# Third stage of a four-block kernel: side work over three banks, probability turning over two, in a new order

## The reference

```python
scores = einsum('bci,bcj->bij', x, x); context = einsum('bij,bcj->bci', softmax(scores), x)   # block 1
mixed = einsum('btd,rde->bte', x, factors) / sqrt(8) + bias                                   # block 2
h = norm_scale * x / (nrm + EPS) * split_scale                                                # block 3
q, k, v = h @ Wq.T, h @ Wk.T, h @ Wv.T      # 8 heads of 64 for q, 2 groups of 64 for k and v
attn = softmax(q k^T / 8); x + (attn v) @ Wo.T
g, u = gate(x) * gate_s, up(x) * up_s; (silu(g) * u) @ down * down_s                          # block 4, inner size 1408
```

## Time and profile before

| what | us |
|---|---|
| median of three runs (lowest, highest) | 1461.83 (1461.3, 1461.9) |
| the profiled execution: its own time | 1460.45 |
| its span | 1458.6 |
| PE, DVE, ACT, POOL busy, share of the span | 95%, 69%, 55%, 51% |
| one batch of block 3 from score to score (batch 3) | 76.6, of it DVE busy 69.67 |

### The profile page before, as it was taken

The page is one execution under the profiler, slowest core; times in us unless marked ns, Lnnn a source line. Parts: engine busy times, 40 slices in busy tenths (PEclk is TensorE's granted clock), DMA queues, the critical chain, the costliest instruction groups (busy, mean ns, idle before and its releaser), DMA issues.

```text
span 1458.6 us, 20717 instructions
## 1 busy us (share of the span) xinstructions
PE 1386.4 (95%) x6864; PEld 1134.4 (78%) x6864; DVE 1010.8 (69%) x2070; ACT 798.1 (55%) x1554; POOL 740.7 (51%) x1008
## 2 busy tenths in 40 slices
PE   5999999988999999999999999799999999999996
PEld 4888877766777877878787887588888888888884
DVE  5888869867989898989898989666242442434333
ACT  4666646647777878786868788632222222213221
POOL 5888646735536465554646455553343424333241
PEclk9999999999999999999999999999999999999998
DMA  6665133241302112121212041430101011010100
GB/s 192 169 174 127 40 101 116 87 130 38 94 4 64 65 44 88 44 87 37 87 28 96 15 121 40 145 138 1 58 1 59 4 54 58 0 58 0 58 29 29
DMA packets 53516, 101.32 MB, mean 69 GB/s; under 512 B 3760, under 2 KB 4784, under 8 KB 53424
## 3 DMA queue, kind: packets, MB, share of 16 engines
q1 hardware_dynamic: 49728, 92.83, 19.1%
q0 software_dynamic: 3696, 7.34, 3.1%
HBM read 70.79 MB, written 25.17 MB: 66 GB/s over the span
## 4 chain that ended last, share of the span: by engine, by line
PE 75%; DVE 13%; POOL 4%; issue 4%; ACT 3%; DMA 1%; SPq 0%; POOLq 0%; DVEq 0%; ACTq 0%
PE context L1889 13%; PE score L2367 11%; PE context L2367 11%; PE context L58 6%; PE score L58 6%; PE context L2395 5%; PE turned L2395 5%; PE score L899 4%; PE turned L1925 4%; PE context L1951 2%; PE context L1953 2%; DVE g_neg_max L1754 2%; PE context L1925 2%; DVE g_q L1677 1%; DVE g_ptl L1770 1%
## 5 line engine op out<-in xcount | busy, mean ns | idle before, releaser
L1413 POOL TENSOR_SCALAR g_prob<-g_prob,g_inv_sum 128x512 f32<-128x512 f32 x256 | 178.0, 697 | 268.9 <-DVE g_inv_sum L1759 268.8
L1548 ACT ACTIVATE g_prob<-score,g_neg_max 128x512 f32<-128x512 f32 x256 | 177.2, 692 | 115.5 <-DVE g_neg_max L1754 113.1
L2143 POOL TENSOR_TENSOR f_hl<-f_hidden,f_hh 128x512 fp32r<-128x512 f32 x88 | 121.9, 1386 | 216.0 <-DVE f_hh L2276 216.0
L1754 DVE TENSOR_REDUCE g_neg_max<-score 128x1 f32<-128x512 f32 x256 | 174.7, 682 | 43.9 <-PE score L58 43.4
L2367 PE MATMUL context<-g_hth,f_w 128*128 128x512 f32 x352 | 137.8, 391 | 2.3 <-ACT f_w L2193 2.2
L2367 PE MATMUL score<-g_hth,f_w 128*128 128x512 f32 x352 | 137.8, 392 | 0.6 <-DVE g_htl L2293 0.5
L2367 PE MATMUL context<-g_htl,f_w 128*128 128x512 f32 x352 | 137.1, 390 | 0.0
L2367 PE MATMUL score<-g_htl,f_w 128*128 128x512 f32 x352 | 137.1, 390 | 0.0
L58 PE MATMUL score<-g_kh,g_q 128*128 128x512 f32 x256 | 123.4, 482 | 10.7 <-ACT g_prob L1548 7.5
L2199 ACT ACTIVATE f_silu<-score,g_bits 128x512 f32<-128x512 f32 x44 | 30.3, 690 | 176.1 <-PE score L2367 176.1
L2199 ACT ACTIVATE f_silu<-context,g_bits 128x512 f32<-128x512 f32 x44 | 30.4, 690 | 174.5 <-PE context L2367 174.5
(11 more groups left out here) (261 smaller groups left out, 3950.6 us busy)
## 6 DMA issues: line engine op xcount, KB each, us to landing
xt<-x_t SPq DMA_DIRECT2D x16, 512.0 KB, 6.9
x_mixed<-x_resident SPq DMA_DIRECT2D x8, 1024.0 KB, 4.4
x_pair<-x_mixed SPq DMA_DIRECT2D x8, 1024.0 KB, 8.2
g_res<-x_mixed SPq DMA_DIRECT2D x8, 1024.0 KB, 6.5
x_attended<-g_res SPq DMA_DIRECT2D x8, 1024.0 KB, 5.1
x_pair<-x_attended SPq DMA_DIRECT2D x8, 1024.0 KB, 5.6
x_resident<-x SPq DMA_DIRECT2D x7, 1024.0 KB, 11.3
factor_sum<-factors POOLq DMA_DIRECT2D x7, 1024.0 KB, 10.8
```

The costliest lines, as they stand in the source:

```text
L1413: nc.gpsimd.tensor_scalar(prob[:, at, :], prob[:, at, :], inv_sum[:, at:at + 1], 1.0, ALU.mult, ALU.mult).then_inc(prob_ready, 1)
L1548: nc.scalar.activation(prob[:, at, :], score[u % 2][:, :], ACT.Exp, bias=neg_max[:, at:at + 1], scale=1.0, accum_out=row_sum[:, at:at + 1] ...
L1754: nc.vector.reduce_max(neg_max[:, at:at + 1], score[u % 2][:, :], AX, negate=True).then_inc(max_ready, 1)
L2143: self.nc.gpsimd.tensor_tensor(self.hl[:, at, :], self.hidden[:, at, :], self.hh[:, at, :].bitcast(F32), ALU.subtract).then_inc(self.hl_re ...
```

## The change

The bank that was the third for turning (`s.output[1]`) becomes the third for side work; turning has two. The order of the names, the shares per step, and some fixed steps are new, and the planner's rule for `earliest` looks back three names instead of two. By hand the new planner ends are: q1 2, v 3, q2 5, q3 8, h0 8, wo0 11, h1 12, wo1 15, h2 15, wo2 18, h3 18, wo3 20, k 23, q0 27, vt 29; wo0 begins in step 9, k in step 21. All steps but 30 and 31 have side work. RESIDUAL goes from (11, 14, 19, 23) to (10, 14, 17, 19), NORM from (19, 20, 28, 29) to (19, 20, 24, 25), ADD is one step behind NORM. CONVERT stays.

```diff
--- before.py
+++ after.py
@@ -1010,25 +1010,25 @@
 
 
 
-NAMES = ["v", "q1", "q2", "q3", "h0", "h1", "wo0", "wo1", "h2", "h3", "wo2", "k", "wo3", "q0", "vt"]
+NAMES = ["q1", "v", "q2", "q3", "h0", "wo0", "h1", "wo1", "h2", "wo2", "h3", "wo3", "k", "q0", "vt"]
 SPLIT = [name for name in NAMES if name[0] != "w"]
-OWN = ("v", "q1", "q2", "q3")
+OWN = ("q1", "v", "q2", "q3")
 IN_LAST = OWN + ("h0", "h1", "h2", "h3")
 
 
 
 FIRST_STATS, FIRST_SCALES = (0, 1, 2, 2), (3, 4)
-STATS = (16, 18, 21, 22)
+STATS = (18, 19, 22, 24)
 SCALES = (31, 0)
-H = (5, 6, 8, 11)
+H = (5, 6, 9, 13)
 CONVERT = (25, 26, 32, 39)
-SHARE, SHARE_AT_END, SHARE_BESIDE_OUT = 8, 7, 3
+SHARE, SHARE_AT_END, SHARE_BESIDE_OUT = 6, 5, 3
 
 LAST_MAP = (0, 1, 2, 3)
 
 PIECES = 3 * IT
 MAP_PIECES = (0, 0, 2, 2, 0, 0, 2, 2)
-STEP_PIECES = [(20, 26, 28, 30)] * 4 + [(20, 28, 30)] * 3
+STEP_PIECES = [(21, 23, 27, 29)] * 4 + [(21, 27, 29)] * 3
 assert sum(MAP_PIECES) + sum(len(steps) for steps in STEP_PIECES) == PIECES
 LOW_COLUMN, LOW_COUNT = 1, 4
 
@@ -1055,7 +1055,7 @@
             name, count = waiting[0]
             cost = 2 if name[0] == "h" or name == "v" else 1
             i = NAMES.index(name)
-            earliest = [end[n] + (2 if n[0] == "w" else 3) for n in NAMES[max(i - 2, 0):max(i - 1, 0)] if n in end]
+            earliest = [end[n] + 3 for n in NAMES[max(i - 3, 0):max(i - 2, 0)] if n in end]
             earliest += {"wo0": [CONVERT[-1] - UNITS + 2], "k": [end.get("h3", 0) + 3],
                          "h0": [H[0] + 2], "h1": [H[1] + 2], "h2": [H[2] + 2], "h3": [H[3] + 2]}.get(name, [])
             if at == 0 and earliest and max(earliest) > u:
@@ -1073,7 +1073,8 @@
 
 
 SHARES, END = side_schedule()
-AHEAD = len(SPLIT) - len(OWN)
+PROLOGUE = [name for name in SPLIT if name not in OWN]
+AHEAD = len(PROLOGUE)
 WO = [END[f"wo{t}"] for t in range(T)]
 RESIDUAL = [at - 1 for at in WO]
 NORM = [WO[1] + 4, WO[1] + 5, WO[3] + 4, WO[3] + 5]
@@ -1086,14 +1087,19 @@
 
 def side_at(b, name):
 
-    return side_use(b, name) % 2
+    return side_bank(side_use(b, name))
+
+
+def side_bank(use):
+
+    return use % 2 if use < AHEAD else 2 - (use - AHEAD) % 3
 
 
 def side_use(b, name):
 
 
     if isinstance(b, int) and b <= 0:
-        return AHEAD + b * len(SPLIT) + SPLIT.index(name)
+        return AHEAD + SPLIT.index(name) if b == 0 else PROLOGUE.index(name)
     j = NAMES.index(name)
     if isinstance(b, int) and b >= B - 1 and name[0] == "w":
         missing = [n for n in NAMES[:j] if n in SPLIT and (b == B or n not in IN_LAST)]
@@ -1103,7 +1109,7 @@
 
 def side_split(b, name):
 
-    return b * len(SPLIT) + (AHEAD + SPLIT.index(name) + 1)
+    return b * len(SPLIT) + (AHEAD + SPLIT.index(name) + 1) if b >= 0 else PROLOGUE.index(name) + 1
 
 
 def side_works(u, first, last, drain):
@@ -1253,8 +1259,8 @@
         obn, omv, ove, ors, oshift = own.obn, own.omv, own.ove, own.ors, own.oshift
         neg_max, row_sum, inv_sum = own.neg_max, own.row_sum, own.inv_sum
 
-        score, side, output = s.score, s.side, s.output[0]
-        turned = [s.turned[0], s.turned[1], s.output[1]]
+        score, side, output = s.score, [s.side[0], s.side[1], s.output[1]], s.output[0]
+        turned = s.turned
         x_loaded = [s.x_first_loaded, sem("x_loaded1")]
         res_loaded, stored = sem("res_loaded"), sem("stored")
         s.attended_stored = stored
@@ -1279,7 +1285,7 @@
 
         def mixed_bank(b, use):
 
-            return (turned if b == B - 1 else side)[use % 2]
+            return turned[use % 2] if b == B - 1 else side[side_bank(use)]
 
         @block.sync
         def _(sp):
@@ -1593,7 +1599,7 @@
                     act.wait_ge(turn_ready, g - TURN_LAG + 1)
                     at = turn_u % T
                     nc.scalar.copy(pth[:, (turn_u // T) % 2, :, at * P:(at + 1) * P],
-                                   blocks_of(turned[(g - TURN_LAG) % 3][:, :])).then_inc(hi_ready, 1)
+                                   blocks_of(turned[g % 2][:, :])).then_inc(hi_ready, 1)
                 for name in side_done(u, first, last, drain, 1):
                     if name in SPLIT:
                         hi_of(b, p, name)
@@ -1757,17 +1763,17 @@
                     at = (u - 1) % 4
                     dve.wait_ge(exp_ready, g)
                     nc.vector.reciprocal(inv_sum[:, at:at + 1], row_sum[:, at:at + 1]).then_inc(inv_ready, 1)
+                if u == END["q0"] + 3 and side_runs("q0", first, last, drain):
+                    lo_of(b, p, "q0", 1)
                 for name in side_done(u, first, last, drain, 2):
                     if name in SPLIT:
                         lo_of(b, p, name, 0 if name == "q0" else None)
-                if u == END["q0"] + 3 and side_runs("q0", first, last, drain):
-                    lo_of(b, p, "q0", 1)
                 turn_u = u - TURN_LAG
                 if not (first and turn_u < 0) and not (drain and turn_u >= 0):
                     dve.wait_ge(hi_ready, g - TURN_LAG + 1)
                     cols = slice(turn_u % T * P, (turn_u % T + 1) * P)
                     at = (turn_u // T) % 2
-                    nc.vector.tensor_tensor(ptl[:, at, :, cols], blocks_of(turned[(g - TURN_LAG) % 3][:, :]),
+                    nc.vector.tensor_tensor(ptl[:, at, :, cols], blocks_of(turned[g % 2][:, :]),
                                             pth[:, at, :, cols].bitcast(F32), ALU.subtract).then_inc(lo_ready, 1)
                 for name in side_done(u, first, last, drain, 1):
                     if name not in SPLIT:
@@ -1835,25 +1841,29 @@
 
         @block.tensor
         def _(pe):
-            def side_bank(use):
-
-                if not (isinstance(use, int) and use < 2):
+            def side_bank_free(b, use):
+
+                if use == AHEAD:
+                    pe.wait_ge(rest.mixed_ready, B * T)
+                elif use > AHEAD and b < B:
+                    pe.wait_ge(side_free, use - 2)
+                elif use >= 2:
                     pe.wait_ge(side_free, use - 1)
 
             def turn_h(b, use, t):
-                side_bank(use)
+                side_bank_free(b - 1, use)
                 pe.wait_ge(h_ready, b * T + t + 1)
                 for k in range(T):
                     cols = slice(k * P, (k + 1) * P)
-                    last = nc.tensor.transpose(side[use % 2][:, cols], h[:, t % 2, cols], s.identity[:, :])
+                    last = nc.tensor.transpose(side[side_bank(use)][:, cols], h[:, t % 2, cols], s.identity[:, :])
                 last.then_inc(side_ready, 1)
 
             def turn_v(b, use):
-                side_bank(use)
+                side_bank_free(b, use)
                 pe.wait_ge(side_hi, side_split(b - 1, "vt"))
                 for t in range(T):
                     cols = slice(t * P, (t + 1) * P)
-                    last = nc.tensor.transpose(side[use % 2][:, cols], v_turned[:, cols], s.identity[:, :])
+                    last = nc.tensor.transpose(side[side_bank(use)][:, cols], v_turned[:, cols], s.identity[:, :])
                 last.then_inc(side_ready, 1)
 
             def split(lh, ll, rh, rl):
@@ -1863,13 +1873,13 @@
 
 
                 use = side_use(b, name)
-                out = mixed_bank(b - 1, use) if name[0] == "w" else side[use % 2]
+                out = mixed_bank(b - 1, use) if name[0] == "w" else side[side_bank(use)]
                 if name[0] == "h":
                     return turn_h(b + 1, use, int(name[1]))
                 if name == "v":
                     return turn_v(b, use)
                 if start == 0:
-                    side_bank(use)
+                    side_bank_free(b, use)
                 if name == "k" and start == 0:
                     pe.wait_ge(side_free, side_use(b, "h3") + 1)
                 if name == "wo0" and start == 0:
@@ -1916,13 +1926,13 @@
                 turn_u = u - TURN_LAG
                 if not (first and turn_u < 0) and not (drain and turn_u >= 0):
                     pe.wait_ge(prob_ready, g - TURN_LAG + 1)
-                    if first and turn_u < 3:
-                        pe.wait_ge(rest.mixed_ready, (B - 1) * T + (1, 2, 4)[turn_u])
+                    if first and turn_u < 2:
+                        pe.wait_ge(rest.mixed_ready, (B - 1) * T + turn_u + 1)
                     else:
-                        pe.wait_ge(lo_ready, g - TURN_LAG - 2)
+                        pe.wait_ge(lo_ready, g - TURN_LAG - 1)
                     for k in range(T):
                         cols = slice(k * P, (k + 1) * P)
-                        mm = nc.tensor.transpose(turned[(g - TURN_LAG) % 3][:, cols], prob[:, turn_u % 4, cols],
+                        mm = nc.tensor.transpose(turned[g % 2][:, cols], prob[:, turn_u % 4, cols],
                                                  s.identity[:, :])
                     mm.then_inc(turn_ready, 1)
                 if not drain:
@@ -1992,7 +2002,7 @@
                 gated.weights_of(pe, 3, with_lo)
```

(9 more changed lines are left out.)

## The result

The changed kernel takes 1482.85 us (median of 4 runs, 1481.19 to 1484.99) against 1461.87 for the kernel before, a ratio of 1.0142, 95% interval 1.0127 to 1.0158: slower by 21 us, nearly twice the 10.9 that the forecast summed up. That is inside the range of eight in ten (1456 to 1484), but only by 1.2, and 1.9 above the forecast's own range of 1465 to 1481. The profiled execution took 1483.15, 22.7 more than that of before.

A forecast was written before the change was run, and what follows sets the result against it. PE was taken as the bound (75.04 of 76.6 us a batch), DVE close behind (69.67). 3 x 0.86 + 3 x 1.78 + 3.0 = 10.9 gave 1471.4 profiled, 1472.7 median; own range 1465 to 1481, eight in ten 1456 to 1484.

The forecast's parts named there:

- The signs: wo0 waiting about 2 us, turns waiting in steps 27 and 0; batches of 78.4 (1 to 3), 77.5 (4 to 6).
- What goes: Five PE waits, at v, the score after step 9, h1 and wo0, h3, wo2, vanish: 3.09 us a batch.
- wo0 in step 9: PE stands 2.07 us before wo0 for the output's last low part, which POOL makes in step 8.
- the 2.80: Time from one DVE maximum to the end of POOL's low part, a term of wo0's wait: 2.80 us.
- DVE's lag at the end: Late DVE makes turns wait for `g_ptl`: 0.73 us in step 27, 1.15 at batch end, 1.88 a batch.
- The piece's transfer: Batches 0 to 3: DVE waits 0.92 us for the third piece's fetch, making the end of batch 2.80.
- rival 4: The clock falls in the new stalls, 1.5 us lost in each of seven batches: 10.5, 1483 us; chance 0.12.
- Batch 7: Score of step 25 comes 3.2 us later behind DVE's lag, before the branch; the batch loses 3.0 in all.
- Batch 0: No wo; stalls of 2.6 us against gains elsewhere: net 0, between -3 and +3.
- Block 4, "and nobody waits for it": Store of the batch before issued some 4 us sooner with nobody waiting for it; block 4 changes 0, within 1.
- The gaps and the banks: Consistent bubbles can mean too few PSUM buffers; by that rule the third side bank wins 3.09 us a batch.
- the prediction's second rule: DVE instructions start only on an empty pipe: plain step 1.51 us, changed kernel near 60 later; forecast rejected it for 1.26.

The follow-up runs named there:

- experiment 2: Changed kernel with POOL's last low part of the output ahead of its normalise in step 8: 1471.88 us, 1.0078 of the kernel before.
- experiment 6: Changed kernel with q2's low part behind the conversion in DVE's step 7: 1501.90 us, 1.0280 of the kernel before.
- experiment 10: Changed kernel with ACT's second norm piece in step 7 instead of 6 and the edit of experiment 6: 1490.29 us, 1.0197 of the kernel before.
- experiment 3: Changed kernel with the statistics five to seven steps sooner (13, 14, 15, 17): 1478.29 us, 1.0130 of the kernel before.
- experiment 4: Changed kernel with half of q0's low part and the count of vt behind `g_ptl` in DVE's step 30: 1475.88 us, 1.0103 of the kernel before.
- Experiment 1: Three side and two turning banks alone, with order, statistics, shares and pieces of the kernel before: 1462.31 us, 1.0010 of the kernel before.
- experiment 5: Changed kernel with the third piece of the next candidates read one step later (28 for 27): 1477.01 us, 1.0108 of the kernel before.
- experiment 11: Changed kernel with only ACT's second norm piece moved from step 6 to step 7: 1480.74 us, 1.0127 of the kernel before.
- experiment 7: Changed kernel with the edits of experiments 2, 3, 4 and 6 together, and the pieces' steps moved too: 1467.48 us, 1.0048 of the kernel before.
- experiment 8: Kernel of experiment 7 with the last batch's weights one to five steps sooner: 1467.91 us, 1.0060 of the kernel before.
- experiment 9: Kernel of experiment 7 without the edit of experiment 6: 1458.07 us over 11 runs, 0.9978 of the kernel before.
- experiment 12: Kernel of experiment 7 with ACT's second norm piece also in step 7: 1462.36 us over 11 runs, 1.0011 of the kernel before.

## Why the prediction was right, and where its sizes were off

The mechanism was right and its sum too small: 10.9 us for 21. That the time still fell inside the range is in part luck. Of what was missing, 4.6 us are the clock, whose rival stood at 0.12, and 1.25 a long issue of two DMAs in batch 1, which the sum had nowhere. The signs came as named, but the batches last 80.8 to 81.1 and 78.4, not 78.4 and 77.5.

**What goes**: right. v, h1, h3 and wo2 start without a bank wait. But the five waits were worth 2.9 a batch by the trace, not 3.09, and small waits of at most 0.1 each, as in steps 8, 9 and 21, which I had counted at nothing, add up to 0.4 to 0.5 in the changed kernel.

**wo0 in step 9**: right in mechanism and size, 1.98 to 2.02 in every batch from 1 to 7 against 2.07. DVE's step 7 took 3.99 (forecast 4.01). Experiments 2, 6 and 10 show the link that holds: POOL's queue, with the normalise ahead of the low part. The forecast had it only as part of the 2.80.

**DVE's lag at the end**: right in kind and place, too small. Step 27 waits 1.19 and 0.15 ahead of it (forecast 0.73), the end 1.89 (2.07 with the piece, 1.15 without; batches 4 to 6 have 0.76 and 1.62). The lag at step 25 was 2.41, forecast 1.84, of which 0.5 comes from step 23, where sum and piece take 2.93, not 2.44: I had the piece at the 0.57 of a pass and took nothing for the instruction ahead. The turn also starts 0.15 behind `g_ptl`, not 0.05, in each of these waits. For batches 4 to 6 I used the demands of four pieces, though they read three, none of them in step 23. Experiments 3 and 4 confirm the two conditions apart from each other: the statistics set step 27, what lies ahead of `g_ptl` in step 30 sets the end.

**The piece's transfer**: 0.92 forecast for batches 0 to 3, 0.4 measured in batches 2 and 3, where DVE itself arrived later. In batch 1 it was 1.7, because the issue of one pair of copies took 2.49 in SP's queue, where the same pair takes 1.24 in batches 0, 2, 3, 4 and 6, and the fetch stood behind it:

```profile
462.74 2.49 SPq L1346 DMA_DIRECT2D g_kl<-g_kl  x2
465.27 0.58 SPq L1160 DMA_DIRECT2D g_h<-down_t  x1
```

**The clock**: rival 4, which I had beside the forecast and not in it, came true in part. Batches 2 and 3 lost 1.6 and 1.7 behind wo0's wait, and batch 7 2.57 in place of 1.22, behind the stall at its branch. (The clock column of batch 7 is 0.98 in some kernels here and 0.96 in others whose stall at the branch is as long, so this part isn't tied to the new waits.) That is 4.6 us of the 12.5 that the sum missed. The rest: batch ends of 1 to 3 2.5, half of it the 1.25 of batch 1; of 4 to 6 1.5; and the terms of "What goes" the remainder.

**Batch 7**: 3.13 in steps 24 and 25 against 3.2. **Batch 0**: 0.15 against 0, by luck. Steps 0 to 6 are 2.3 shorter than before and steps 7 and 8 2.7 longer, and neither was in the forecast.

**Block 4, "and nobody waits for it"**: this step failed, by 2.2 to the good. In the kernel before PE waits in block 4 for weights that were fetched late:

```profile
943.54 0.50 PE L2367 MATMUL context<-g_hth,f_w 128*128 128x512 f32 x1 [2.17 <-ACT f_w L2193]
```

The fetches stand in SP's queue behind the stores of block 3; the changed kernel issues those sooner. Before, then after (last scores of block 3 at 928.3 and 953.1):

```profile
929.99 0.40 SPq L1291 DMA_DIRECT2D x_attended<-g_res  x1
934.38 0.38 SPq L1346 DMA_DIRECT2D g_res<-x_mixed  x1
934.80 0.58 SPq L2112 DMA_DIRECT2D raw_w<-gate_t  x1
```

```profile
945.45 0.40 SPq L1297 DMA_DIRECT2D x_attended<-g_res  x1
949.83 0.38 SPq L1352 DMA_DIRECT2D g_res<-x_mixed  x1
953.85 0.35 SPq L2123 DMA_DIRECT2D raw_w<-gate_t  x1
```

The fetch comes 6.5 behind the last score before and 0.7 behind it after, and the wait is gone in every kernel here with the new order, and stays with the banks alone.

**The gaps and the banks.** Four of the five gaps looked like too few banks, as the Trainium skill (Perfetto Trace Analysis, Optimization Strategy) allows. Experiment 1 gives the third bank and moves the gaps to the turns: by the trace the buffers were one limit, and DVE's lateness the next, worth as much (2.4 of waits for 2.1). As to the prediction's second rule, the section that it names (VectorE: DVE Perf Modes, The DRAIN you can't avoid) says in the same paragraph that a next instruction which isn't held starts earlier; so the 1.26 of a plain DVE step doesn't contradict the Trainium skill, and the 60 us worked out from that rule had no ground.

## What to carry to other kernels

A buffer taken from one stage for another moves the wait, as long as the engine that frees both is late; first ask how late that engine is, step by step. An instruction ahead of a critical one may be filling a wait that is there anyway: moving it behind can cost nearly its whole length (1.36 of 1.39 here), so look up what the critical one waits for before moving anything. Work late in one engine's order can wait on a chain that runs over another queue's older entries, and then reordering that queue is the cure, as with POOL's two instructions here, worth about 11 us.

## What the runs showed of the hardware

- The same wait of 2.0 us was followed by about 1.6 us lost at 1.2 GHz in batches 2 and 3 and by nothing in batches 1 and 4 to 7 of one execution. Over the five profiles with this wait (the changed kernel and experiments 3, 4, 5 and 11) it was 10 batches of 35. With wo0's wait at 0.7 or less (experiments 2, 7, 8, 9 and 12) no batch showed it there, with 2.85 (experiment 10) four of seven did, and with 3.6 (experiment 6) all seven. A stall of 2 us on PE has a price that varies by 1.6.
- The issue of two DMAs took SP's queue 1.11 us for `g_kh` and 1.24 for `g_kl` right behind it in most batches, but for `g_kl` 2.49 and 2.60 in batches 1 and 5 of the changed kernel and 2.68 and 2.15 in batches 2 and 5 of the kernel before. The profiles of experiments 1, 2 and 6 have none of these. The cause stayed open.
- Executions of most kernels in which wo0 waits 2.0 or more spread more: over four runs each 6.5 us in experiment 5 (1474.6 to 1481.2) and 7.0 in experiment 11, and 2.8 to 5.0 in the other five, against 3.7 in 21 runs of the kernel before (1458.8 to 1462.5).
